# One wide eviction for two narrow ones, and a layernorm apply without its helper value

## The reference

```
xn  = layernorm(x)                       # over 1024, eps 1e-5
Q, K, V = xn@W1+b1, xn@W2+b2, xn@W3+b3
att = softmax(Q K^T / 32) V @ W4 + b4
ffn = complex linear map of xn: real and imaginary halves of 512,
      weights unfolded from G1 (1,32,4,32) and G2 (4,16,1,16)
return x + att + ffn
```

## Time and profile before

| | us |
|---|---|
| median of 2 runs | 1649.44 |
| the two runs | 1637.73, 1661.15 |
| profiled execution, device time | 1659.86 |
| its span on core 1, the slowest | 1658.2 |
| spans of the other cores | 1624.1 to 1654.7 |

### The profile page before, as it was taken

The page is one execution under the profiler, slowest core; times in us unless marked ns, Lnnn a source line. Parts: engine busy times, 40 slices in busy tenths (PEclk is TensorE's granted clock), DMA queues, the critical chain, the costliest instruction groups (busy, mean ns, idle before and its releaser), DMA issues.

```text
span 1658.2 us, 24155 instructions; the slowest of 8 cores (1624.1 to 1658.2 us)
## 1 busy us (share of the span) xinstructions
PE 1537.9 (93%) x8496; PEld 772.6 (47%) x8496; DVE 732.7 (44%) x1495; ACT 484.8 (29%) x881; POOL 80.6 (5%) x75
## 2 busy tenths in 40 slices
PE   0599999998999999999999999999999999999998
PEld 0354656664444444444444444444444444444443
DVE  0423223333455355535553555355355535553544
ACT  0132333442223322323323222322322322333322
POOL 1100111111000000000000000000000000000000
PEclk9998889998999999999999999999999999999999
DMA  9722112125111111111101111111011111110001
GB/s 156 137 29 62 52 52 75 54 77 134 33 53 50 39 39 39 39 39 39 43 34 39 52 39 39 39 39 64 26 38 52 39 39 39 39 39 26 26 26 39
DMA packets 69524, 83.41 MB, mean 50 GB/s; under 512 B 39699, under 2 KB 49947, under 8 KB 69406
## 3 DMA queue, kind: packets, MB, share of 16 engines
q1 hardware_dynamic: 56030, 42.01, 9.1%
q10 hardware_dynamic: 9216, 33.56, 6.3%
q0 software_dynamic: 4160, 6.29, 2.6%
HBM read 69.27 MB, written 18.87 MB: 53 GB/s over the span
## 4 chain that ended last, share of the span: by engine, by line
PE 91%; DVE 3%; DMA 3%; issue 2%; SPq 1%; ACT 0%; POOL 0%; DVEq 0%; ACTq 0%; POOLq 0%
PE po L663 14%; PE po L667 13%; PE po L563 13%; PE sp_a L563 7%; PE sp_b L563 7%; PE sp_a L420 4%; PE sp_b L420 4%; PE pf L594 4%; PE po L444 3%; PE sp_a L530 3%; PE pf L444 3%; PE sp_b L530 3%; PE ptA L634 2%; PE po L294 2%; PE pf L604 2%; PE pf L599 2%
## 5 line engine op out<-in xcount | busy, mean ns | idle before, releaser
L663 PE MATMUL po<-V,ETs 128*128 128x512 bf16 x1024 | 387.9, 379 | 14.5 <-DVE ETs L646 14.5
L667 PE MATMUL po<-V,ETs 128*128 128x512 bf16 x1024 | 388.0, 379 | 0.0
L563 PE MATMUL po<-KT,QXT 128*128 128x512 bf16 x1024 | 231.5, 379 | 0.0
L624 DVE TENSOR_REDUCE r<-Et 128x1 f32<-128x512 bf16 x256 | 173.8, 679 | 31.6 <-ACT Et L620 31.4
L620 ACT ACTIVATE Et<-Ssb,ngm 128x512 bf16<-128x512 f32 x256 | 164.2, 709 | 57.3 <-DVE ngm L584 47.2
L563 PEld LDWEIGHTS po<-KT,QXT 128*128 128x128 bf16 x1024 | 100.2, 98 | 120.8
L663 PEld LDWEIGHTS po<-V,ETs 128*128 128x128 bf16 x1024 | 100.0, 98 | 113.7 <-issue 19.1
L576 DVE TENSOR_REDUCE mx<-po 128x1 f32<-128x512 f32 x128 | 88.6, 692 | 132.7 <-ACT Ssb L573 132.7
L375 POOL TENSOR_SCALAR xnn<-xg,rstd,nmr 128x1024 bf16<-128x1024 f32 x64 | 76.1, 1194 | 1408.1 <-DVE nmr L371 1408.1
L667 PEld LDWEIGHTS po<-V,ETs 128*128 128x128 bf16 x1024 | 100.0, 98 | 94.5
L573 ACT ACTIVATE Ssb<-sp_a 128x512 f32<-128x512 f32 x64 | 38.2, 597 | 351.7 <-PE sp_a L563 351.7
(11 more groups left out here) (90 smaller groups left out, 1595.3 us busy)
## 6 DMA issues: line engine op xcount, KB each, us to landing
xg<-x ACTq DMA_DIRECT2D x64, 512.0 KB, 3.6
xr<-x SPq DMA_DIRECT2D x32, 512.0 KB, 3.5
out<-xr SPq DMA_DIRECT2D x32, 512.0 KB, 2.6
KT<-W POOLq DMA_DIRECT2D x2, 2048.0 KB, 39.1
Ssb<-W SPq DMA_DIRECT2D x8, 512.0 KB, 7.7
Wproj<-W POOLq DMA_DIRECT2D x1, 2048.0 KB, 21.6
scr<-V SPq DMA_DIRECT2D x2, 1024.0 KB, 6.9
V<-scr SPq DMA_DIRECT2D x64, 32.0 KB, 2.9
```

The lines of the kernel that those rows point to most:

```text
L563: P.add("tensor", lambda e, tb=tb, c=c, si=si, spv=spv: e.matmul(spv, QT[:, c, si * 128:(si + 1) * 128], KT[:, c, tb * 512:(tb + 1) * 512] ...
L624: P.add("vector", lambda e, tb=tb: e.reduce_sum(r8[:, tb:tb + 1], Et[:, tb % 4, :], axis=AX.X), waits=[("exp", i, tb)] + ([("rr", i - 1)] ...
L663: P.add("tensor", lambda e, tb=tb, q=q, tj=tj: e.matmul(po[:, 0:512], ETs[:, tb % 4, q, :], V0[:, tj, 0:512], start=(tj == 0), stop=(tj == ...
L667: P.add("tensor", lambda e, tb=tb, q=q, tj=tj: e.matmul(po[:, 512:1024], ETs[:, tb % 4, q, :], V0[:, tj, 512:1024], start=(tj == 0), stop= ...
```

## The change

Two edits.

First, in the W3' product the two evictions of 512 columns per m become one of 1024 columns. It is recorded after both halves of m, waits for both, and both halves of m+1 wait for it. What waited for ("W3pe", 7, 1) waits for ("W3pe", 7).

Second, `nmr` goes. POOL computes (x - mean)·rstd from `bn2` and `rstd`, and waits for `rstd` (ACT) in place of `nmr` (DVE).

```diff
-                               ("W3pe", m - 1, h) if m > 0 else
+                               ("W3pe", m - 1) if m > 0 else
                                 ("Gev", 1, 6 + h)],
                         mark=("W3pm", m, h) if k == 7 else None)
-                P.add("scalar", lambda e, m=m, h=h: e.activation(
-                    W3p[:, m, h * 512:(h + 1) * 512],
-                    po[:, h * 512:(h + 1) * 512], AF.Identity),
-                    waits=[("W3pm", m, h)], mark=("W3pe", m, h))
-        free["po"] = ("W3pe", 7, 1)
-        W3PDONE = ("W3pe", 7, 1)
+            P.add("scalar", lambda e, m=m: e.activation(
+                W3p[:, m, :], po[:, :], AF.Identity),
+                waits=[("W3pm", m, 0), ("W3pm", m, 1)], mark=("W3pe", m))
+        free["po"] = ("W3pe", 7)
+        W3PDONE = ("W3pe", 7)
...
-        P.add("vector", lambda e, s=s: e.tensor_scalar(
-            nmr[:, s, :], bn2[:, s, 0:1], rstd[:, s, 0:1], -1.0,
-            ALU.mult, ALU.mult),
-            waits=[("rstd", gt)], mark=("nmr", gt))
         P.add("gpsimd", lambda e, s=s: e.tensor_scalar(
-            xnn[:, s, :], xg[:, s, :], rstd[:, s, 0:1], nmr[:, s, 0:1],
-            ALU.mult, ALU.add),
-            waits=[("nmr", gt), ("xtp", gt - 2, 1) if gt >= 2 else None],
+            xnn[:, s, :], xg[:, s, :], bn2[:, s, 0:1], rstd[:, s, 0:1],
+            ALU.subtract, ALU.mult),
+            waits=[("rstd", gt), ("xtp", gt - 2, 1) if gt >= 2 else None],
             mark=("lnap", gt))
```

More of the change, by code:

```diff
@@ L430, in emit_khalf @@
             elif full and g in (4, 5):
-                kw.append(("W3pe", 7, 1))
+                kw.append(("W3pe", 7))
             elif full and g in (6, 7):
-                kw += [("W3pe", 7, 1), ("cbm", 1)]
+                kw += [("W3pe", 7), ("cbm", 1)]
             P.add("scalar", lambda e, c=c, g=g, spv=spv, off=off: e.activation(
```

## The result

| | before | after |
|---|---|---|
| median (executions) | 1657.82 us (10) | 1669.27 us (11) |
| lowest | 1635.77 us | 1667.37 us |
| profiled execution | 1659.86 us | 1667.55 us |

The ratio, in which disturbed executions are left out, is 1.0123, 95% interval 1.0069 to 1.0176: slower by 1.2%, where the medians of the table differ by 0.7%. The forecast was 1650 us with 1669 as its upper end; the median lies 0.3 us beyond it.

What follows compares the result with a forecast made beforehand. The prediction took PE's queue of matmuls as the bound. Wide eviction +9.9 us, start -9.1 (core 5 -8.0) and behind the product -0.8 gave 0.0 to +1.1 us on a 1649.4 us median: 1650 us, range 1635 to 1669 us.

Steps and rivals of the forecast that it cites:

- POOL's price: POOL's subtract and multiply for `xnn`: taken as 1.19 us a tile as before, at most twice that.
- the start and tiles 6 and 7: The places said to lose up to 2.4 us each if POOL's operation took twice 1.19 us.
- Rival D: POOL's new operation for `xnn` is dearer, over 1.3 us; up to 2.4 us lost at each place named; chance 0.05.
- Edit 1's cost: W3' product: PE waits for the wide eviction in seven holes of 1.41 us, +9.9 us.
- Edit 2's gain at the start: Before the K projection: POOL no longer queues behind `nmr`, loads go earlier; -9.1 us core 1, -8.0 us core 5.
- Rival A: Start: late loads shrink the gain, +4.5 to +9 us, 1654 to 1659 us; chance 0.13.
- about 4: Sign of being right: PE's wait for `xnn` at the start falls from 12 to about 4 us.
- Rival B: W3' product: the seven holes put PE at 1.2 GHz, 27.7 us more, 1678 us; chance 0.04.
- The rule of the Trainium skill: Brief PE idling between matmul groups cycling through PSUM can make its clock swing between two levels; weighed for the product.
- Rival C: W3' product: holes keep core 1 at full clock, saving 25 us, median 1639 us; chance 0.10.
- The sum: Edits cancel: core 1 +9.9 - 9.1 - 0.8 = 0.0 us, core 5 +1.1 us; forecast 1650 us; chance 0.66.

Runs made afterwards that it cites:

- edit 2 alone: Kernel before with only `nmr` removed (POOL subtract, multiply), evictions narrow: 1670.25 us, ratio 1.0202.
- the cheap form: `nmr` removed with the new order and wait, narrow evictions, but POOL keeps multiply and add (normalisation wrong): 1642.89 us, ratio 0.9992; 1629.9 us at full clock.
- edit 1 alone: Kernel before with only the wide eviction, `nmr` kept: 1649.37 us, ratio 1.0069.
- the narrow kernel: Kernel before with DVE negating the mean early and POOL doing add, then multiply, evictions narrow; rerun on the last chip: 1651.96 us, ratio 0.9989.

## Why the prediction was wrong, and where it was right

**The step that failed: POOL's price.** The prediction said that no row shows subtract and multiply on POOL and took the 1.19 us of before; as the far end it set twice that, and for its reach "the start and tiles 6 and 7". Both were off. The price is 3.78 us, 3.2 times the old one. That alone would have been a larger loss at the places named. Most of the loss came from the second error, the reach. In the K and V projections POOL starts two tiles 1.35 us after the V matmuls do (180.33 and 178.98), and TensorE wants the second at 186.49. With 0.35 us for the hand-over that leaves (186.49 - 180.33 - 0.35) / 2 = 2.9 us for a tile. At 1.19 us, and at the far end of 2.4 us too, the work is hidden; at 3.78 us it is late by 2 x 0.87 us with every pair of tiles, twice in a group. That PE never waits for `xnn` there was true at the old price, and how much of a price it would bear was never worked out, although the trace of before had both sides, here on core 5:

```profile
162.17 3.62 PE L444 MATMUL po<-Ssb,QXT 128*128 128x512 bf16 x16
...
163.85 2.37 POOL L375 TENSOR_SCALAR xnn<-xg,rstd,nmr 128x1024 bf16<-128x1024 f32 x2 [11.04 <-DVE nmr L371]
...
170.25 0.38 PE L395 MATMUL ptA<-ident,xnn 128*128 128x128 bf16 x4 [0.56 <-DVE QXT L400]
```

PE is ready for the second tile at 169.69 us, 5.84 us behind POOL's start: less 0.35 us, 2.7 us for a tile. Rival D named the right operation and a sixth of its cost.

In the stages of core 5: at the start the queue gave its 8 us and the form took 6.7 in edit 2 alone, 9.4 in after (+1.4 instead of -8.0); behind the product the form took 20 us (+18.9, where the cheap form has -1.5). The 20 us are twelve waits of 1.73 us, 20.8 us, and the longer ones at tiles 6 and 7, less the waits for copies to `xnT` (8.6 us in 15 in the run with the cheap form) that they swallowed, plus a K half behind tile 7 that takes 0.8 us longer (153.97 to 162.17 us before, 169.90 to 178.89 after), one more group at the lower clock level. I have not brought these parts to an exact sum.

The Trainium skill (GPSIMD Engine Reference, 3.1 Elementwise - side-by-side cycle accounting) measures about 2.6 cycles an element for `tensor_tensor` add and puts that down to its two input tensors; its best case for a loop is about 1.8 cycles. At the 1.2 GHz it uses, 1024 elements would be an estimated 2.2 us by the first figure and 1.5 us by the second, which is nearer to this operation with its one input tensor. The rows have 1.19 us, below both, and 2.84 and 3.78 us, above both, and one operation dearer than two of the cheap sort; the measurement decides.

**Edit 1's cost: right.** Forecast 1.41 us for each of seven holes, 9.9 us; measured 4.88 - 3.46 = 1.42 us and +10.0 us on core 5, +10.4 us in the times of edit 1 alone. The idle part was to be 1.2 to 1.3 us and is 1.26, the last eviction is hidden behind the bias matmuls as said.

**Edit 2's gain at the start: right, but only in the run with the cheap form** (-8.0 and -8.7 for -8.0 and -9.1). Rival A falls with it: the loads had landed, DVE did not wait for tile 2, and between the first K matmul and the product TensorE had no wait that before did not have. In after, TensorE's long waits for `xnn` at the start came to 7.42 and 4.18 us where "about 4" was forecast.

**Rival B: refuted.** The product's matmuls are 379 ns on average in after and the clock of all cores of its profile is 0.994 and more. The rule of the Trainium skill that the prediction weighed (TensorE: Matmul & The Clock Gate, "A second HAM failure mode: psum-queue depth-cycling") does not show here: seven idle holes of 1.26 us at a pitch of 4.88 us left the clock at 1.00. The lower level did come in after, but behind the waits of 2.99 and 2.75 us at tiles 6 and 7. That the clock was also lost at the start, as the prediction says in weighing that rule, rests on the pace of the first K matmuls alone, as the granted clock reads 1.00 there.

**Rival C: happened, and had 0.10.** It said that holes may keep the product's core from the stretch at 0.8, with 25 us as its worth. None of the 37 executions of the four kernels with wide evictions is of the sort "pairs", and 40 of the 82 executions of before in the table are. (One of the 37, of add, then multiply, wide, at 1877.4 us, has cores 0 and 1 at 0.98 and 0.979 beside four cores at 0.85 to 0.864; it is counted under "other".) The argument against it, that other cores ran the same block at full clock, was weak: the low clock hits one pair of cores in one execution and another in the next, and the time is that of the slowest core. So what hits one or two pairs of cores decides the time of half the executions. It is worth 20 to 23 us (on the last chip before goes from 1637.0 to 1660.2, the narrow kernel from 1631.6 to 1651.7), where the prediction took 25.

**The sum.** Forecast 0 to +1; at equal clock it is +30.7 us by the stages of core 5: 10.0 for edit 1, -7.9 for the order (the run with the cheap form has 329.4 us from the first copy to the Q projection, before 337.3), and the 28.6 us that remain for POOL's form. The medians show +11 because the low stretch of about 20 us went from the executions that had it. The forecast also stood on 1649.4 us, the middle of two executions, where ten give 1657.8: of the 19.3 us between forecast and median, 8.4 are that base. The missed price of POOL's form and the missed rival C have opposite signs, so the median lies only 0.3 us outside the range; that is luck, and the wrong step is not smaller for it.

**What stays open.** Why one pair falls and its neighbours do not is not settled: no run changed the neighbours. Nothing between three and seven breaks was tried, and the breaks were tried in this product alone. Whether a one-column matmul counts as a break because of its narrow operand or for another reason was not tried. Nor was why POOL's forms cost what they do, or why the low stretch ends: the runs give prices and lengths alone.

**A better kernel.** Add, then multiply on POOL with the bias matmuls between narrow evictions takes 1630.9 us against 1660.1 of before on the same chip, and 1632.3 against 1639.6 on another: about 6 us better at full clock (1632.2 to 1638.1, 1630.7 to 1637.1). Of its 20 executions 16 are at full clock, one has a pair at 0.979, and three are of the sort "other".

## What to carry to other kernels

An operation with other arithmetic at the same size isn't the same operation: where no row prices it, work out at which price its cover is gone, at each place where it runs, and let the range reach there; or keep to a form that the trace has priced (here: negate once on a small tile, then add). Where the slowest of several cores is timed, a disturbance that hits few of them sets the median, so compare cores and executions at the same clock before a difference is put down to an edit. A stretch of matmuls that loses clock may keep it when work of another shape is put into it, which cost nothing here, as that work had to be done anyway.

## What the runs showed of the hardware that was not expected

POOL's `tensor_scalar`, 128 x 1024 float32 to bf16: 1.19 us for two operations without subtract (multiply and add, add and multiply, multiply twice), 2.84 us for one operation alone, 3.78 to 3.79 us for two with subtract in either place.

The granted clock of 0.81 comes on pairs of cores (0 and 1, 2 and 3, 4 and 5, 6 and 7), from one pair to three in one execution. It begins 5.6 to 7.8 us into the unbroken product and lasts 160 to 161 us on each of the twelve low cores of the profiles that have it, over three to four slices of 41 us. The Trainium skill (TensorE: Matmul & The Clock Gate, Part 1) has this level, 13/16, for a whole die; in the 40 executions of before it is one pair (26) or two (14), and in 35 of them the other pair of such a die stands at full clock, as in the earlier trace rows.

Seven breaks in 32 us of full-width matmuls kept it away, three did not. Of 67 executions with seven breaks 52 are at full clock, 2 have such pairs and 13 are of the sort "other"; with three breaks it is 3, 6 and 1, without breaks, in before, 34, 40 and 8.
